# Weight preparation drained from the first step on, group 0 prepared ahead of group 1, and every second projection copy moved to VectorE

## What is computed

```python
encR = jnp.einsum('bnd,de->bne', encoding, R)
scores = jnp.einsum('bnd,bmd->bnm', encR, encoding)
A = jax.nn.softmax(scores + mask, axis=2)        # causal mask
x = _layernorm(x + jnp.einsum('bnm,bmd->bnd', A, encoding))
h = bitlinear(x, W1, b1)
h = jax.nn.gelu(h, approximate=False)
x = _layernorm(x + bitlinear(h, W2, b2))
```

## Time and profile before

| | |
|---|---|
| median of three runs | 2563.1 us |
| lowest and highest of the three | 2507.2 and 2614.2 us |
| profiled execution, its own time | 2504.6 us |
| its span on the slowest core (core 6) | 2503.1 us |
| spans of the eight cores | 2491.6 to 2503.1 us |
| mean granted TensorE clock | 0.904 to 0.917 of 2.4 GHz |
| busy: PE, PEld, DVE, ACT, POOL | 1848.5, 798.9, 975.5, 641.9, 174.0 us |

### The profile page before, as it was taken

How to read it: one execution, slowest core, us unless ns; L and a number is a source line. 1 busy time by engine, 2 the same in 40 slices (tenths; PEclk the granted TensorE clock), 3 DMA queues, 4 the chain that set the end, 5 groups by cost and what they waited for, 6 DMA issues and landing times.

```text
span 2503.1 us, 27365 instructions; the slowest of 8 cores (2491.6 to 2503.1 us)
## 1 busy us (share of the span) xinstructions
PE 1848.5 (74%) x8840; PEld 798.9 (32%) x9016; DVE 975.5 (39%) x1941; ACT 641.9 (26%) x1271; POOL 174.0 (7%) x307
## 2 busy tenths in 40 slices
PE   0168678787887975107999889999898998998930
PEld 0023233343333432002333333333333333333310
DVE  0033241323232333335454454545545455454422
ACT  0022222232232321003223232332323323232210
POOL 2010111101121111110000000000000000000000
PEclk9998899999998997558999999999999999999975
DMA  8866646535656455574000000000000000000038
GB/s 137 173 179 199 185 168 177 185 106 145 123 135 154 101 148 127 131 218 150 26 13 26 19 20 26 13 26 13 26 26 13 26 13 26 26 13 26 5 125 287
DMA packets 124603, 233.82 MB, mean 93 GB/s; under 512 B 52140, under 2 KB 52268, under 8 KB 123438
## 3 DMA queue, kind: packets, MB, share of 16 engines
q0 software_dynamic: 43408, 129.24, 20.8%
q1 hardware_dynamic: 66016, 88.14, 11.2%
q10 hardware_dynamic: 15040, 14.68, 2.2%
HBM read 166.21 MB, written 69.21 MB: 94 GB/s over the span
## 4 chain that ended last, share of the span: by engine, by line
PE 57%; DMA 23%; issue 8%; DVE 6%; ACT 4%; SPq 2%; POOL 1%; DVEq 0%; ACTq 0%; POOLq 0%
PE psc L757 16%; PE pav L827 9%; PE pav L823 9%; DMA w2q_h<-f_big 6%; PE psc L546 5%; PE ptp L575 4%; DMA bf_med<-r_bfT 4%; PE psc L531 3%; PE psc L763 3%; PE pav L592 3%; DMA w1q_h<-f_big 3%; PE pav L598 3%; DMA bf_med<-y2pre_h 3%; ACT bf_med L582 2%; DMA f_big<-w1t 2%
## 5 line engine op out<-in xcount | busy, mean ns | idle before, releaser
L757 PE MATMUL psc<-bf_big,bf_med 128*128 128x512 bf16 x1984 | 484.6, 383 | 10.9 <-DMA bf_big<-w1q_h 6.8
L827 PE MATMUL pav<-bf_big,bf_med 128*128 128x512 bf16 x1023 | 396.7, 388 | 4.4 <-ACT bf_med L582 1.3
L823 PE MATMUL pav<-bf_big,bf_med 128*128 128x512 bf16 x977 | 379.2, 388 | 1.0 <-ACT bf_med L582 0.9
L531 PE MATMUL psc<-bf_big,bf_med 128*128 128x512 bf16 x502 | 154.5, 468 | 214.1 <-DMA bf_med<-r_bfT 204.8
L546 PE MATMUL psc<-bf_big,bf_med 128*128 128x512 bf16 x1127 | 280.8, 390 | 1.6 <-issue 0.4
L575 PE MATMUL ptp<-ident,bf_med 128*128 128x128 bf16 x1808 | 170.0, 222 | 131.3 <-ACT bf_med L582 64.6
L768 ACT ACTIVATE f_big<-psc,stats 128x512 f32<-128x512 f32 x256 | 176.0, 687 | 345.7 <-PE psc L763 338.2
L772 DVE TENSOR_REDUCE stats<-f_big 128x1 f32<-128x512 f32 x256 | 169.5, 683 | 233.3 <-ACT f_big L768 233.3
L757 PEld LDWEIGHTS psc<-bf_big,bf_med 128*128 128x128 bf16 x2048 | 181.5, 98 | 239.9 <-issue 57.9
L559 ACT ACTIVATE bf_med<-psc,stats 128x512 bf16<-128x512 f32 x144 | 99.1, 689 | 387.3 <-DVE psc L554 190.8
L575 PEld LDWEIGHTS ptp<-ident,bf_med 128*128 128x128 bf16 x1808 | 118.2, 98 | 208.5 <-issue 177.2
(11 more groups left out here) (112 smaller groups left out, 1544.6 us busy)
## 6 DMA issues: line engine op xcount, KB each, us to landing
f_big<-w1t POOLq DMA_DIRECT2D x64, 512.0 KB, 5.7
f_big<-w2t POOLq DMA_DIRECT2D x64, 512.0 KB, 5.1
f_big<-enc POOLq DMA_DIRECT2D x32, 512.0 KB, 7.0
bf_med<-r_bfT SPq DMA_DIRECT2D x64, 256.0 KB, 4.2
y1pre_h<-f_big SPq DMA_DIRECT2D x32, 512.0 KB, 2.9
f_big<-y1pre_h POOLq DMA_DIRECT2D x32, 512.0 KB, 3.9
out<-f_big SPq DMA_DIRECT2D x32, 512.0 KB, 3.9
bf_big<-enc POOLq DMA_DIRECT2D x36, 256.0 KB, 11.8
```

Of the source, the lines that this page charges most:

```text
L531: lambda t, e=e, d=d, cur=cur, qlo=qlo, bk=bk: t.matmul(psc[bk][:, :], Rcol(cur)[:, 128 * d:128 * (d + 1)], efm(d, qlo, qlo + 512), start= ...
L757: b.op("tensor", lambda t, d=d, s4=s4, sup=sup: t.matmul(psc[s4][:, :], xq_fm[:, 128 * d:128 * (d + 1)], w1tb(d)[:, 512 * sup:512 * (sup + ...
L823: b.op("tensor", lambda t, c=c: t.matmul(pav[:, 0:512], hq_fm[:, 128 * c:128 * (c + 1)], w2tb(c)[:, 0:512], start=(c == 0), stop=False), r ...
L827: b.op("tensor", lambda t, c=c: t.matmul(pav[:, 512:1024], hq_fm[:, 128 * c:128 * (c + 1)], w2tb(c)[:, 512:1024], start=(c == 0), stop=False),
```

## The change

There are three edits. The start of the program treats group 0 of the tiles before group 1, where it was group 1 before group 0, and puts the loads of group 2 between the first R column and the stores of group 1. The projection copies of e = 1, 3, 5 and 7 go from ScalarE to VectorE. The fractions of the weight preparation are (2 oi + 1) / 64 and (oi + 1) / 32 instead of (2 oi - 3) / 60 and (oi - 1) / 30, without a floor at zero.

```diff
--- before.py
+++ after.py
@@ -367,14 +367,14 @@
                   r_bfT[:, :, 128 * d:128 * (d + 1)].transpose([1, 0, 2]),
                   stg.rearrange("p (e j) -> p e j", e=8),
                   reads=[rg], accum_writes=["rbfT"])
+        emit_enc_loads(0)
         emit_enc_loads(1)
-        emit_enc_loads(0)
+        emit_enc_stores(0)
+        emit_enc_transp(0)
+        b.dma("sync", Rcol(0), r_bfT[0], reads=["rbfT"], writes=["Rcol0"])
+        emit_enc_loads(2)
         emit_enc_stores(1)
         emit_enc_transp(1)
-        b.dma("sync", Rcol(0), r_bfT[0], reads=["rbfT"], writes=["Rcol0"])
-        emit_enc_stores(0)
-        emit_enc_transp(0)
-        emit_enc_loads(2)
         emit_enc_loads(3)
         emit_enc_stores(2)
         b.dma("gpsimd", eres(0), enc[128 * order[0]:128 * (order[0] + 1), :],
@@ -534,8 +534,14 @@
                              start=(d == 0), stop=(d == 7)),
                          reads=[f"Rcol{cur}", f"efm{d}g{m}"],
                          writes=[f"psc{bk}"], inc=(d == 7))
-                b.op("scalar", lambda s, e=e, bk=bk: s.copy(encR(e), psc[bk][:, :]),
-                     reads=[f"psc{bk}"], writes=[f"encR{e}"])
+                if e % 2 == 0:
+                    b.op("scalar", lambda s, e=e, bk=bk: s.copy(
+                        encR(e), psc[bk][:, :]),
+                        reads=[f"psc{bk}"], writes=[f"encR{e}"])
+                else:
+                    b.op("vector", lambda v, e=e, bk=bk: v.tensor_copy(
+                        encR(e), psc[bk][:, :]),
+                        reads=[f"psc{bk}"], writes=[f"encR{e}"])
 
         def emit_scores_super(qi, sup, p):
             nsup = (qi + 4) // 4
@@ -660,8 +666,8 @@
             if oi < NT:
                 emit_softmax_tail(qi, par)
             if oi >= 1:
-                drain_prep(max(0.0, (2.0 * oi - 3.0) / (2.0 * (NT - 2))))
-            drain_prep(max(0.0, (oi - 1.0) / (NT - 2.0)))
+                drain_prep((2 * oi + 1) / (2.0 * NT))
+            drain_prep((oi + 1) / (1.0 * NT))
         drain_prep(1.0)
 
         b.barrier()
```

## The result

The changed kernel is slower, by less than 2% but clear of the noise: the ratio of its undisturbed runs to those of the kernel before is 1.0132, with a 95% interval of 1.0110 to 1.0154. Of 2507 us that is 33 us. Its profiled execution took 2534.95 us with a span of 2533.4 us on core 6, against 2504.6 and 2503.1 us. Some executions show the cores of a die at a lower clock; the comparisons leave these out, and so ratios are given and not medians.

A forecast was written before the change was run, and what follows sets the result against it. Attention half held by the start, weight preparation (DVE's and POOL's queues) and the chunk tail; window shifts, with +5, +13, +1 for copies and -6.9 for the tail, sum to about +6 us: 2569 us, range 2500 to 2615.

The forecast's parts named there:

- the forecast's own band: Whole kernel: result within about 10 us of the forecast +6 us; chance 0.45.
- the first rival in part: Projections of steps 20, 24, 28: copies chain PE to weight preparation, partly; +16 to +50 us, chance 0.17.
- the tail: End of the attention half, after the last steps: one weight-preparation chunk less runs alone; -6.9 us.
- Window 19: Loop window after step 18: four chunks instead of five, paced by POOL's queue at 31.1 us a step; -0.8 us.
- The order: Program start, group 0 before group 1: e = 0 runs later, e = 1 doesn't move; 0, bounds -1 and +16 us.
- the four steps that drain only sums: Steps 4, 8, 12, 16: sums end before e = 3 starts, so the copies cost 0.
- the term of the copies: Odd copies behind chunks in VectorE's queue hold e = 3: +5, +13, +1 us in steps 20, 24, 28.
- rival 1: Steps 20, 24, 28: copies chain PE to the preparation, nothing caught up afterwards; +54 us, chance 0.05 in full.
- Rival 2: POOL's queue, first store to 1095 us: quantising starts earlier and keeps its lead; -20 us, chance 0.15.
- The late start: Program start: transposes slower with e = 0 behind them, or e = 1 waits too; +16 us on top, chance 0.08.
- The rule on descriptors: GpSimd can't write descriptors during DVE two-port operations; if copies did this, at most 0.42 us each, sum +8 not +6.
- The prediction's reading of its two issues: POOL's issues in the quantising half: 0.95 us beside DVE's arithmetic and 0.53 alone, taken as agreeing with the descriptor lock.

## Why the prediction was right or wrong

The forecast was +6 us, the result +33 us. It is inside the range and within 2%, and more than the forecast's own band; the first rival in part (+16 to +50) is what happened, to which 0.17 was given. The number itself, 2569 us, stands beside a median of 2568.1 us over the ten runs of the changed kernel, and that is luck: it was built on the 2563.1 us of three runs of the kernel before, whose ten runs have a median of 2507.1.

**Right, by place and size.** Most windows outside the projections came as worked out: windows 1 to 3 +12.3 us together (forecast +11), 7 to 10 without the projection of step 8 -6.8 (forecast -8.7), 21 to 23 84.1 us (forecast 84.1), the tail 6.8 us shorter (forecast 6.9). Window 19 did not: it was put at -0.8 us, though the prediction's own pace of 31.1 us a step is above its 30.1, and it took 32.7. All that is not the copies was forecast at 6 - 19 = -13 us; the fractions alone measured 0.9949, -13 us, and with the order at the start 0.9970, -8 us. The order was forecast at 0 and measured 0.9994; e = 1 stayed at 117 us. e = 3 starts right behind the last L459 and the copy in steps 20 and 24, 28.1 and 35.7 us after the epilogue where 27.2 and 34 were worked out, and the four steps that drain only sums hold nothing.

**Wrong: the term of the copies.** It was +5, +13 and +1, together +19 us. The kernel with everything but the copies (0.9970) and the changed kernel (1.0132) differ by 1.6%, 41 us; from the fractions alone (0.9949) it is 1.8%, 46 us. So the term was under half of what it is. The mechanism was right, and two sizes in it were not: how long the holds are, and how much of a hold is caught up behind it. The forecast holds here are worked out from the times in the prediction, and a cost is that of the whole window, measured against the fractions alone:

| | hold, forecast | hold, measured | cost, forecast | cost, measured |
|---|---|---|---|---|
| step 20 | 13.4 us | 11.6 us | +5 us | +11.3 us |
| step 24 | 19.3 us | 24.9 us | +13 us | +20.7 us |
| step 28 | 4.7 us | 10.0 us | +1 us | +6.0 us |
| together | 37 us | 46.6 us | +19 us | +38 us |

About half of the missing 19 us are longer holds. In step 24 e = 3 could start 10.8 us after the epilogue, not 14.7, and the chunks ended 1.3 us later than worked out. In step 28 the prediction let four chunks end 17.8 us after the epilogue at 952.66, for which it shows no row; they ended after 22.4:

```profile
974.33 0.75 DVE L459 TENSOR_SCALAR f_big<-f_big,stats 128x1024 f32<-128x1024 f32 x1
975.00 0.68 DVE L542 CAST bf_med<-psc 128x512 bf16<-128x512 f32 x1
```

The other half is the stretch behind the holds: of 37 us the forecast had 18 caught up, of 46.6 us there were 9. The prediction let groups 3 and 4 run at once and gave 5 to 7 "reloads of about 3 us each", 12.7 us in all. It took 18.5 and 19.5 us, the stretches of steps 20 and 24 in the columns used above:

```profile
648.27:666.80 18.53, 12.88 (x40) 4.64 (x42) 1.38 (x2) 1.17 (x2) 2.11 (x4) 0.78 0.80 189
811.60:831.20 19.60, 14.36 (x41) 5.13 (x43) 1.38 (x2) 1.17 (x2) 2.10 (x4) 0.69 0.65 183
```

Two things are in there. PE waits 5.6 and 5.2 us for columns, where 12.7 us leave 3.3 beside five groups of 1.89. A column lands in about 4 us (the median of 3.9; the page of the kernel before has 4.2), not in 3; e = 5 starts 8.1 us behind e = 3, and e = 7 another 8.5 us behind e = 5. And PE comes out of the hold at the lower clock level: in the row at 648.27 the 16 matmuls take 5.92 us, and 16 at full clock 3.6. The five groups are busy for 12.9 and 14.4 us and not for 9.45. So of what the forecast lacks here, 2.4 and 2.0 us are columns and 3.4 and 4.9 us the clock. Against the kernel before the clock is less, since its projections ran partly at the lower level too: L531 is busy for 160.3 us in the page of the changed kernel and 154.5 before. The run with three buffers took most of the column waits out of step 20, with the hold in place, and the five groups came to 12.4 us.

Window by window, the changed kernel stands above the fractions alone by 11.3 us in window 20, 20.7 in 24, 6.0 in 28, and 2.2 each in 8 and 19, together 42 us. Window 28 was forecast at +1 also because I compared the end of the chunks with where e = 3 had started in the trace of before; but with four chunks instead of five, and no copies behind them, that window falls to 54.4 us, a gain that the copies took away. The 2.2 us of windows 8 and 19 stand beside no wait for a copy and are not settled.

**The rivals.** The chain of PE to the preparation was named as rival 1 with the three steps in which it bites, and it is the cause; "nothing is caught up afterwards" is wrong as it stands, but little is, 9 us of 46.6. Rival 2, the earlier start kept to the end, is out: the tail is the chunks that the fractions leave, as the prediction said. The late start is out. The rule on descriptors can be answered in part: two issues of POOL in the changed kernel, the first beside L456 and L459, the second beside the copy at 647.45.

```profile
646.62 1.03 POOL L110 DMA_DIRECT2D f_big<-w1t  x1 [5.67 <-DMA w1q_h<-f_big]
647.64 0.54 POOL L110 DMA_DIRECT2D w1q_h<-f_big  x1
```

The load took 1.03 us beside the arithmetic from SBUF, the store 0.54 us beside the copy out of PSUM, as stores do with VectorE idle. The prediction's reading of its two issues was wrong, though: the one that took 0.53 us, at 602.55, was not alone but beside the last two operations of a chunk. Taken over the whole attention half of that trace, the 44 loads issued beside no VectorE operation took 0.53 to 0.55 us, and 29 beside a chunk's operations 0.53 to 1.03, with a median of 0.95. The Trainium skill, page "SBUF — State Buffer", in the box on the trap in which DVE blocks DMA, ties the lock to two-port operations. The trace of the changed kernel agrees as far as it goes: the three issues that stood beside a copy out of PSUM alone took 0.53 and 0.54 us, no longer than beside nothing. The Trainium skill, page "VectorE: DVE Perf Modes", in the section on the TRN2 errata, gives 0.66 us for such a copy by its formula; the median of the 32 copies is 0.692 us, and the measurement decides.

## What to carry to other kernels

Before moving an eviction (the copy that empties a PSUM bank) to another engine, look at what stands ahead of it in that engine's queue at that moment, and not at the engine's busy share: VectorE was 39% busy and ScalarE 26% in the kernel before, and PE was held by neither's speed but by chunks that were waiting for loads. Don't count on a hold being caught up behind it: here 38 of 46.6 us stayed, since the next loads start only behind the held group (each lands in about 4 us) and its matmuls run at the lower clock (16 in 5.92 us and not 3.6). And an order of this kind can be used the other way round: copies that stand ahead of the chunks keep the chunks' transfers out of the projection. With three buffers the move of the chunks alone gained nothing (0.9734 against 0.9739), and with the copies on VectorE, except behind the last chunks, it came to 0.9687. With two buffers the move of the chunks was not run without the copies, so how much of 0.9915 is due to them is not shown.

## What had not been expected

The order of work in VectorE's queue set the speed of transfers in SP's. With the same bytes and two buffers, the R columns landed in 4.2 us in the kernel before and in 3.1 us where the copies stood ahead of the chunks. With three buffers they landed in 5.3 and 4.7 us (by buffer) where nothing held the chunks back, and in 3.3 and 3.2 us where the copies did. So the copies on VectorE, which cost 1.6 to 1.8% in the change, belong to the fastest version.
